# The low part of the token tiles: from a VectorE subtraction to a ScalarE negation and an adding transfer

## The chip, the cores and the metric

One core of one Trainium2 chip runs the kernel. The metric is device time in microseconds (us) of one execution; of the kernel before three runs are given.

## What is computed

The reference takes x of shape 32 x 64 x 1024 (2048 tokens, D = 1024), runs it through a linear map with a gated low-rank addition (8 experts, rank 16, two of them chosen per token), runs the result through a second linear map with another gated low-rank addition (4 experts, rank 8), and adds x. Cut to what matters:

```python
base = einsum('btd,od->bto', x, W)
logits = einsum('btd,ed->bte', x, Wr) + one_hot(language) * 5
topw, topi = top_k(logits, 2); gates = one_hot(topi) . softmax(topw)
h = einsum('btd,erd->bter', x, A)
c = base + 2 * einsum('bter,bte,eor->bto', h, gates, B)
...
gates2 = softmax(einsum('bsi,ei->bse', c, Wr2))
out = x + einsum('bsi,oi->bso', c, W2) + b + 2 * sum_e gates2 * (c A2_e^T Bm_e^T)
```

## The kernel before

The two maps are first multiplied into one (C, with the identity added), which takes about the first 99 us. Then the 2048 tokens go through in 16 tiles of 128, two at a time: eight **pairs**, pair 0 to pair 7. Pairs 0 and 1 have bodies of their own, pairs 2 to 6 are a loop (one body, in which every engine keeps its own order of instructions, written out by hand), pair 7 has the loop's body without what prepares a next pair.

Accuracy comes from splitting. A float32 tile is rounded to the format that TensorE takes (its **high** part), the rest is the **low** part, and a product is three matmuls: high by high, high by low, low by high. So TensorE needs `st_high` and `st_low` of both tiles of a pair (index `odd`, 0 or 1; below "x0" and "x1"), each 128 x 1024, and of four sums and differences of their halves (`s_plain`, hence `s_high` and `s_low`), since a Strassen-like scheme of seven products (P1 to P7) replaces eight.

How a token tile of pair j+1 comes to be, all of it during pair j:

- SP loads it from `tokens` in HBM into `stage[:, odd, :]` (`load_pair`, L461 to L466). It waits until VectorE has made all four sums of the pair that is in `stage` (`s_made`) and until the tile there has been split (`x_split[odd]`). Its transfers x0 and x1 are followed on the same queue by the two stores of the pair (`store`, L468 to L475), which wait for the additions into `rows`.
- ScalarE rounds it, `round_x` (L599 to L601, the copy itself is at L549): x0 once product 2 of pair j is through, x1 once product 4 is.
- VectorE subtracts, `split_x` (L883, the operation itself is at L800), and counts up `x_split[odd]`.
- TensorE uses both parts of pair j+1 from `narrow_products` on (L1494 to L1518), with which a pair of the loop begins: seven products with 244 columns (12 matmuls each), in the order P1n, P6n, P2n, P7n, P5n, P4n, P3n. P1n and P2n read x0; **P4n is the first to read x1**. The wide products with 354 columns follow. In the kernel before, `narrow_products` waits on `x_split[0]` ahead of P1n; ahead of P4n there is only the wait on a sum that VectorE makes later than the split of x1.

```python
pe.wait_ge(x_split[0], j + 1)                                     # ahead of P1n
...
pe.wait_ge(u3n_read, j - 1)                                       # ahead of P4n
narrow_of_x(BANK_NB, 1, 1, tn_high[T4], tn_low[T4], False)
```

POOL (GpSimd) builds a few constants in the first 60 us and then has nothing.

Of the kernel before, what the change touches and what calls it, by code (L numbers as in the profile page):

```python
# [5 lines left out]
def adaln_ffn_kernel(nc, part_2, part_1, part_3, part_4, tokens, gate_proj, mix_rows, language, out):  # L6
# [16 lines left out]
    ALU = mybir.AluOpType  # L23
    ACT = mybir.ActivationFunctionType
# [8 lines left out]
    PAIRS = TILES // 2  # L33
# [56 lines left out]
    with ctx:  # L90
# [3 lines left out]
        def sem(name):  # L94
            return ctx.enter_context(nc.semaphore(name))
# [43 lines left out]
        stage = sb("stage", [P, 2, D])  # L139
# [19 lines left out]
        st_low = sb("st_low", [P, 2, KC, P], F32R)  # L159
# [145 lines left out]
        x_here = [sem("x_here_0"), sem("x_here_1")]  # L305
        x_rounded = [sem("x_rounded_0"), sem("x_rounded_1")]
        x_split = [sem("x_split_0"), sem("x_split_1")]
        s1_made = sem("s1_made")
        s_made = sem("s_made")
        s_rounded = sem("s_rounded")  # L310
# [130 lines left out]
        def sync_program(sp):  # L441


            sp.dma_start(in_2[:, 0, 2 * P:ROWS_A], part_2[0, :, 2 * P:ROWS_A]).then_inc(here_2_first[0], 16)
            sp.dma_start(in_2[:, 0, 0:2 * P], part_2[0, :, 0:2 * P]).then_inc(here_2[0], 16)
            for k in range(1, HALF):
                sp.dma_start(in_2[:, k, :], part_2[k]).then_inc(here_2[k], 16)
            for k in range(HALF):
                sp.dma_start(in_1[:, k, :], part_1[k]).then_inc(here_1[k], 16)
            for k in range(HALF):  # L450
                sp.dma_start(in_3[:, k, :], part_3[k]).then_inc(here_3[k], 16)
            for k in range(HALF):
                sp.dma_start(in_4[:, k, :], part_4[k]).then_inc(here_4[k], 16)
            sp.dma_start(gate_in, gate_proj.rearrange("p k c -> p (k c)")).then_inc(gate_here, 16)
            sp.dma_start(mix_in, mix_rows).then_inc(mix_here, 16)
            sp.dma_start(lang_i[:, :], language).then_inc(lang_here, 16)

            for odd in range(2):
                sp.dma_start(rows[:, odd, :], tokens[odd]).then_inc(x_here[odd], 16)

            def load_pair(j):  # L461

                sp.wait_ge(s_made, 4 * j)
                for odd in range(2):
                    sp.wait_ge(x_split[odd], j)
                    sp.dma_start(stage[:, odd, :], tokens[2 * j + odd]).then_inc(x_here[odd], 16)  # L466

            def store(j):  # L468
                sp.wait_ge(tails_out, j + 1)
                sp.wait_ge(a_out, j + 1)  # L470
                sp.wait_ge(c_out, j + 1)
                sp.dma_start(out[bass.ds(2 * j * P, P), :], rows[:, 0, :]).then_inc(stored[0], 16)
                sp.wait_ge(b_out, j + 1)
                sp.wait_ge(d_out, j + 1)
                sp.dma_start(out[bass.ds((2 * j + 1) * P, P), :], rows[:, 1, :]).then_inc(stored[1], 16)  # L475

            def store_last(j):


                def block_out(t, h):  # L480
                    at = stored_at(h)
                    return sp.dma_start(out[(2 * j + t) * P:(2 * j + t + 1) * P, at], rows[:, t, at])

                def tail_out(t):
                    return sp.dma_start(z_of(out[(2 * j + t) * P:(2 * j + t + 1) * P, :], STORED, HZ),
                                        z_of(rows[:, t, :], STORED, HZ))

                sp.wait_ge(tails_out, j + 1)
                tail_out(0).then_inc(stored[0], 16)
                tail_out(1).then_inc(stored[1], 16)  # L490
                sp.wait_ge(d_out, j + 1)
                block_out(1, 1).then_inc(stored[1], 16)
                sp.wait_ge(b_out, j + 1)
                block_out(1, 0).then_inc(stored[1], 16)
                sp.wait_ge(c_out, j + 1)
                block_out(0, 1).then_inc(stored[0], 16)


            sp.wait_ge(s_split, 4)
            load_pair(1)  # L500


            sp.wait_ge(cw_split, 3)
            sp.wait_ge(t_split, 4)
            for c in (C11, C12, C22, C21):
                k = HALF if c in (C21, C22) else 0
                a = GH if c in (C12, C22) else 0
                sp.dma_start(c_plain[:, c, :, GATE_AT:WIDE], gate_proj[:, k:k + HALF, a:a + GH])\
                    .then_inc(gate_again, 16)
            with sp.Fori(0, PAIRS - 2) as j:  # L510
                load_pair(j + 2)
                store(j)
            store(PAIRS - 2)
            store_last(PAIRS - 1)

        def gpsimd_program(pool):
            nc.gpsimd.memset(ident[:, :], 0.0).then_inc(ident_made, 1)
            pool.wait_ge(ident_made, 1)
            nc.gpsimd.affine_select(out=ident[:, :], in_=ident[:, :], compare_op=ALU.not_equal, fill=1.0,
                                    base=0, pattern=[[-1, P]], channel_multiplier=1).then_inc(ident_made, 1)  # L520
            nc.gpsimd.iota(expert_no[:, :], pattern=[[1, E1]], base=0, channel_multiplier=0,
                           allow_small_or_imprecise_dtypes=True).then_inc(expert_made, 1)

            nc.gpsimd.memset(mix_is_low[:, :], 0.0).then_inc(mask_made, 1)
            pool.wait_ge(mask_made, 1)
            nc.gpsimd.memset(mix_is_low[2 * ER2:3 * ER2, :], 1.0).then_inc(mask_made, 1)
            pool.wait_ge(mask_made, 2)
            nc.gpsimd.affine_select(out=mix_is_low[:, :], in_=mix_is_low[:, :], compare_op=ALU.not_equal, fill=1.0,
                                    base=-(MIX - 1), pattern=[[0, 1]], channel_multiplier=1).then_inc(mask_made, 1)
            pool.wait_ge(mask_made, 3)  # L530
            nc.gpsimd.tensor_scalar(mix_sign[:, :], mix_is_low[:, :], -2.0, 1.0, ALU.mult, ALU.add)\
                .then_inc(mask_made, 1)


            pool.wait_ge(lang_here, 16)
            nc.gpsimd.tensor_copy(lang_f[:, :], lang_i[:, :]).then_inc(lang_made, 1)
            pool.wait_ge(lang_matched, 1)
            nc.gpsimd.tensor_scalar(lang_bias[:, :, :], lang_bias[:, :, :], LANG_BIAS, None, ALU.mult)\
                .then_inc(lang_made, 1)

        def scalar_program(act):

# [5 lines left out]
            def copy(out_, in_):  # L548
                return nc.scalar.activation(out_, in_, ACT.Copy)  # L549
# [49 lines left out]
            def round_x(j, odd, x=stage):  # L599
                act.wait_ge(x_here[odd], 16 * j + 16)  # L600
                copy(st_high[:, odd, :, :].rearrange("p k c -> p (k c)"), x[:, odd, :]).then_inc(x_rounded[odd], 1)  # L601

            def round_s(j, n, plain=s_plain):
                act.wait_ge(s_made, 4 * j + S_MADE[n])
# [16 lines left out]
            for p in range(2):  # L621
                last = copy(c0_sum[:, CUT[p]:CUT[p + 1]], rt_sums(p))
# [74 lines left out]
            def pair(j, first=False, second=False, last=False):  # L697
                steady = not first and not second
# [17 lines left out]
                for t in range(2):  # L716
                    ins = nc.scalar.activation(pair_exp[:, t:t + 1], top[:, t, 0:1], ACT.Exp, bias=top[:, t, 1:2],  # L717
                                               scale=-1.0)
# [13 lines left out]
                if steady and not last:  # L732
                    act.wait_ge(p2_done, j + 1)
                    round_x(j + 1, 0)

                if steady and not last:
                    act.wait_ge(u_half_turned, j - 1)
# [16 lines left out]
                if not steady:  # L754
                    act.wait_ge(p2_done, j + 1)
                    round_x(j + 1, 0)

                act.wait_ge(v_turned, j + 1)
                copy(vt[2 * ER2:3 * ER2, :, :], vt_plain[0:ER2, :, :])
# [9 lines left out]
                if not last:  # L769
                    act.wait_ge(p4_done, j + 1)  # L770
                    round_x(j + 1, 1)

                if not first:
                    act.wait_ge(stored[0], 16 * j)
# [6 lines left out]
                    round_next(j + 1, S1, p5_done)  # L781

            pair(0, first=True)
            pair(1, second=True)
            with act.Fori(2, PAIRS - 1) as j:
                pair(j)
# [6 lines left out]
        def vector_program(dve):  # L793
# [291 lines left out]
            def pair(j, first=False, second=False, last=False):  # L1085
# [181 lines left out]
                    add_r22()  # L1267
                if second:
                    split_tn(T4)
                if not last:  # L1270
                    split_x(j + 1, 0)
                if first:
                    next_s(S1)
# [16 lines left out]
                add_sums(rows[:, 1, wide_at(0)], bank(BANK_B), rows[:, 1, wide_at(0)]).then_inc(b_out, 1)  # L1290
                if turning:
                    split_s(j + 1, S3)
                if not last:
                    split_x(j + 1, 1)
                if first:
                    split_s(j + 1, S2)
# [11 lines left out]
        def tensor_program(pe):  # L1308
# [89 lines left out]
            for n in range(2, STEPS_F):  # L1398
                q, k = of_step(n)
# [58 lines left out]
            def narrow_of_x(n, odd, h, b_high, b_low, fresh):  # L1458
                return narrow_product(n, st_high, st_low, (odd, h * HALF), b_high, b_low, fresh)
# [33 lines left out]

            def narrow_products(j):  # L1494

                pe.wait_ge(x_split[0], j + 1)
                narrow_of_x(BANK_NA, 0, 0, cn_high[B11], cn_low[B11], True).then_inc(p1n_done, 1)

                pe.wait_ge(s_split, 4 * j + S_NO[S2])
# [11 lines left out]
                narrow_of_s(BANK_NC, S1, tn_high[T1], tn_low[T1], True).then_inc(p5n_done, 1)  # L1511

                pe.wait_ge(u3n_read, j - 1)
                narrow_of_x(BANK_NB, 1, 1, tn_high[T4], tn_low[T4], False).then_inc(p4n_done, 1)

                pe.wait_ge(s_split, 4 * j + S_NO[S4])
# [189 lines left out]
```

## Time and profile before

| | |
|---|---|
| median of 3 runs | 323.37 us (322.85, 323.37, 323.40) |
| the profiled execution, span of the core's instructions | 321.9 us |
| difference of the two | 1.5 us |
| TensorE busy | 318.2 us (99%) |
| VectorE busy | 262.5 us (82%) |
| ScalarE busy | 128.2 us (40%) |
| GpSimd busy | 11.3 us (3%) |
| DMA, packets of the transfers queue | 23.5% of 16 engines' span |
| length of one pair of the loop | 27.0 to 27.1 us |

The span is the time from the core's first to its last recorded instruction in one profiled execution; the runs are timed around it, so they are longer by what lies before and after. Busy times of different engines overlap. PE is TensorE's matmul, PEld its weight load, DVE is VectorE, ACT ScalarE, SP and SPq the engine that issues most transfers.

### The profile page before, as it was taken

The numbers are of one execution on the slowest core, as the hardware profiler recorded it, in microseconds if no ns is written. First come the engines' busy times: TensorE is split into PE (matmuls) and PEld (weight loads), VectorE is DVE, ScalarE is ACT, GpSimd is POOL, SyncE is SP. The second block draws the span as 40 slices with busy tenths as digits, with TensorE's granted clock in tenths as the row PEclk, the third lists the DMA queues.
The fourth block names the chain that finished last, engine by engine and source line by source line (L and its number), as shares of the span: only waits on it lengthen the run. The fifth ranks groups of instructions, "written<-read, shape, count | busy, mean of one in ns | idle before, by whom it ended". The sixth has DMA issues, their size and how long they took to land.

```text
span 321.9 us, 5996 instructions
## 1 busy us (share of the span) xinstructions
PE 318.2 (99%) x2246; PEld 311.9 (97%) x2246; DVE 262.5 (82%) x609; ACT 128.2 (40%) x258; POOL 11.3 (3%) x13
## 2 busy tenths in 40 slices
PE   8999999999999999999999999999999999999996
PEld 5999999999999899899999999999999999999996
DVE  3999999798799778988968968878895987888543
ACT  3872836495147236325412503421251350333111
POOL 1001003700000000000000000000000000000000
DMA  7999000000000312700330150051025006002003
GB/s 266 419 404 290 3 2 0 2 0 2 0 2 0 132 24 46 260 3 0 109 154 1 60 201 0 0 191 70 0 74 187 0 21 239 0 0 110 24 0 130
DMA packets 10704, 27.59 MB, mean 86 GB/s; under 512 B 3166, under 2 KB 4702, under 8 KB 10688
## 3 DMA queue, kind: packets, MB, share of 16 engines
q1 hardware_dynamic: 10256, 26.83, 23.5%
q10 hardware_dynamic: 432, 0.53, 0.5%
q8 instruction: 11, 0.18, 0.2%
q14 instruction: 5, 0.04, 0.0%
HBM read 18.97 MB, written 8.39 MB: 85 GB/s over the span
## 4 chain that ended last, share of the span: by engine, by line
PE 98%; DMA 1%; DVE 0%; issue 0%
PE sums L1310 98%; DMA in<-part 1%; PE sums L1571 0%; DVE rows L1069 0%; DVE b_high L806 0%
## 5 line engine op out<-in xcount | busy, mean ns | idle before, releaser
L1310 PE MATMUL sums<-b_high,a_high 128*128 128x256 f32 (+1 forms) x224 | 45.3, 286 | 0.3 <-DVE b_high L806 0.3
L1310 PE MATMUL sums<-b_low,a_high 128*128 128x256 f32 (+1 forms) x224 | 45.2, 286 | 0.0
L1310 PE MATMUL sums<-b_high,a_low 128*128 128x256 f32 (+1 forms) x224 | 45.0, 286 | 0.0
L1310 PEld LDWEIGHTS sums<-b_high,a_high 128*128 128x128 f32 x224 | 34.7, 189 | 1.0 <-ACT a_high L549 0.8
L1310 PEld LDWEIGHTS sums<-b_low,a_high 128*128 128x128 f32 x224 | 34.7, 189 | 0.0
L1310 PEld LDWEIGHTS sums<-b_high,a_low 128*128 128x128 f32 x224 | 34.6, 188 | 0.0
L1310 PE MATMUL sums<-t_high,s_high 128*128 128x354 f32 x96 | 31.3, 326 | 0.0
L1310 PE MATMUL sums<-t_low,s_high 128*128 128x354 f32 x96 | 31.1, 324 | 0.0
L1310 PE MATMUL sums<-t_high,s_low 128*128 128x354 f32 x96 | 31.1, 324 | 0.0
L1069 DVE TENSOR_TENSOR rows<-sums,rows 128x354 f32<-128x354 f32 x48 | 24.4, 522 | 4.1 <-PE sums L1310 3.4
L1310 PE MATMUL sums<-ct_low,st_high 128*128 128x244 f32 (+1 forms) x80 | 25.6, 320 | 0.0
L1310 PE MATMUL sums<-ct_high,st_high 128*128 128x244 f32 (+1 forms) x80 | 25.6, 320 | 0.0
L1310 PE MATMUL sums<-ct_high,st_low 128*128 128x244 f32 (+1 forms) x80 | 25.5, 318 | 0.0
L717 ACT ACTIVATE pair_exp<-top 128x1 f32<-128x1 f32 x16 | 3.8, 287 | 47.9 <-DVE top_at L1157 47.8
L1069 DVE TENSOR_TENSOR narrow<-sums,narrow 128x244 f32<-128x244 f32 x30 | 12.3, 409 | 12.6 <-PE sums L1310 12.6
L1310 PE MATMUL sums<-c_high,st_high 128*128 128x354 f32 x64 | 21.0, 327 | 0.0
L1310 PE MATMUL sums<-c_high,st_low 128*128 128x354 f32 x64 | 20.8, 324 | 0.0
L1310 PE MATMUL sums<-c_low,st_high 128*128 128x354 f32 x64 | 20.7, 324 | 0.0
L800 DVE TENSOR_TENSOR b_low<-in,b_high 128x530 fp32r<-128x530 f32 (+2 forms) x29 | 19.9, 685 | 0.0
L1082 DVE STREAM_TRANSPOSE narrow<-u 32x64 f32<-32x64 f32 x80 | 18.8, 235 | 1.1
L549 ACT ACTIVATE s_high<-s_plain 128x512 fp32r<-128x512 f32 x28 | 16.7, 624 | 7.0 <-PE sums L1310 6.4
L800 DVE TENSOR_TENSOR s_low<-s_plain,s_high 128x512 fp32r<-128x512 f32 x28 | 18.9, 685 | 0.2
(151 smaller groups left out, 845.8 us busy)
## 6 DMA issues: line engine op xcount, KB each, us to landing
stage<-tokens SPq DMA_DIRECT2D x14, 512.0 KB, 4.0
out<-rows SPq DMA_DIRECT2D x14, 512.0 KB, 4.9
in<-part SPq DMA_DIRECT2D x7, 585.0 KB, 8.8
in<-part SPq DMA_DIRECT2D x4, 777.0 KB, 14.0
in<-part SPq DMA_DIRECT2D x4, 265.0 KB, 16.4
rows<-tokens SPq DMA_DIRECT2D x2, 512.0 KB, 13.6
out<-rows SPq DMA_DIRECT2D x3, 192.0 KB, 2.3
c_plain<-gate_proj SPq DMA_DIRECT2D x1, 544.0 KB, 18.0
```

Source lines behind the costliest of these rows:

```text
L549: return nc.scalar.activation(out_, in_, ACT.Copy)
L717: ins = nc.scalar.activation(pair_exp[:, t:t + 1], top[:, t, 0:1], ACT.Exp, bias=top[:, t, 1:2], scale=-1.0)
L800: return nc.vector.tensor_tensor(dst, src, as_f32(high), ALU.subtract)
L1069: return nc.vector.tensor_tensor(dst, n, onto, ALU.add)
L1082: ins = nc.vector.transpose(ut_plain_at(at, q * BLOCK, BLOCK), u[rows_at, :, at])
L1310: return nc.tensor.matmul(out_, lhs, rhs, start=start, stop=stop, skip_group_check=True)
```

## The change

In pairs 1 to 6, which prepare pairs 2 to 7, the low part is no longer made by VectorE. ScalarE, right after it has rounded a token tile, writes minus the tile, rounded as the high part is, into `st_low`: `negate_x` is a Copy with scale -1 from `stage` into the rounded format. Then GpSimd issues a transfer that reads the same tile from `tokens` in HBM once more and adds it onto `st_low` (`accum_op=ADD`), which leaves x minus rounded x. TensorE waits for that transfer (`x_added`). SP's next load waits for the negation in place of the subtraction. Pair 0 is as before, and with it the tiles of pairs 0 and 1. The rest of the difference unrolls one turn of SP's loop.

```diff
-            def load_pair(j):
+            def load_pair(j, steady=False):
                 sp.wait_ge(s_made, 4 * j)
                 for odd in range(2):
-                    sp.wait_ge(x_split[odd], j)
+                    sp.wait_ge(x_negated[odd] if steady else x_split[odd], j)
                     sp.dma_start(stage[:, odd, :], tokens[2 * j + odd]).then_inc(x_here[odd], 16)
...
-            with sp.Fori(0, PAIRS - 2) as j:
-                load_pair(j + 2)
+            load_pair(2)
+            store(0)
+            with sp.Fori(1, PAIRS - 2) as j:
+                load_pair(j + 2, steady=True)
                 store(j)
...
+            for j in range(2, PAIRS):
+                for odd in range(2):
+                    pool.wait_ge(x_negated[odd], j + 1)
+                    pool.dma_start(st_low[:, odd, :, :].rearrange("p k c -> p (k c)"), tokens[2 * j + odd],
+                                   accum_op=ALU.add).then_inc(x_added[odd], 16)
...
+            def negate_x(j, odd):
+                nc.scalar.activation(st_low[:, odd, :, :].rearrange("p k c -> p (k c)"), stage[:, odd, :], ACT.Copy,
+                                     scale=-1.0).then_inc(x_negated[odd], 1)
...
                     act.wait_ge(p2_done, j + 1)
                     round_x(j + 1, 0)
+                    negate_x(j + 1, 0)
...
                     act.wait_ge(p4_done, j + 1)
                     round_x(j + 1, 1)
+                    if not first:
+                        negate_x(j + 1, 1)
...
-                if not last:
+                if first:
                     split_x(j + 1, 0)
...
-                if not last:
+                if first:
                     split_x(j + 1, 1)
...
             def narrow_products(j):
-                pe.wait_ge(x_split[0], j + 1)
+                pe.wait_ge(x_added[0], 16 * (j - 1))
...
                 pe.wait_ge(u3n_read, j - 1)
+                pe.wait_ge(x_added[1], 16 * (j - 1))
                 narrow_of_x(BANK_NB, 1, 1, tn_high[T4], tn_low[T4], False).then_inc(p4n_done, 1)
```

ScalarE's order in the loop's body, from the rounding of x1 to the body's last rounding; before (names are out<-in; the semaphores waited for in brackets):

```order
L549 ACTIVATE vt<-vt_plain 32x256 [waits v_turned]
L549 ACTIVATE vt<-vt_plain 32x256
L604 REGISTER_ALU [waits p7_done]
L549 ACTIVATE s_high<-s_plain 128x512 [waits s_made]
L549 ACTIVATE st_high<-stage 128x1024 [waits x_here_1,p4_done]
L549 ACTIVATE rows<-sums 128x354 [waits a_done,stored_0]
L549 ACTIVATE s_high<-s_plain 128x512 [waits s_made,p5_done]
```

And of the change:

```order
L560 ACTIVATE vt<-vt_plain 32x256 [waits v_turned]
L560 ACTIVATE vt<-vt_plain 32x256
L620 REGISTER_ALU [waits p7_done]
L560 ACTIVATE s_high<-s_plain 128x512 [waits s_made]
L560 ACTIVATE st_high<-stage 128x1024 [waits x_here_1,p4_done]
L616 ACTIVATE st_low<-stage 128x1024
L560 ACTIVATE rows<-sums 128x354 [waits a_done,stored_0]
L560 ACTIVATE s_high<-s_plain 128x512 [waits s_made,p5_done]
```

The negation stands between the rounding of x1 and the copy of product A into `rows`, which everything after it on ScalarE now follows by one instruction more.

TensorE's waits in the narrow products of a loop pair, of the change (the rows between, without waits, are left out by "..."):

```order
L1334 MATMUL sums<-ct_high,st_high 128x244 [waits x_added_0]
...
L1334 MATMUL sums<-ct_high,s_high 128x244 [waits s_split]
...
L1334 MATMUL sums<-ct_high,st_high 128x244 [waits r1n_read]
...
L1334 MATMUL sums<-t_narrow,st_high 128x244 [waits x_added_1,u3n_read]
...
L1334 MATMUL sums<-ct_high,s_high 128x244 [waits r22n_read,s_split]
```

The transfer of x0 is waited for by the first matmul of the pair, that of x1 by the first of P4n, five products later. No matmul moved.

## Rows read from the trace of the kernel before

**Rows 1.** The page's list of engines, and its chain that ended last
```profile
PE 318.2 (99%) x2246; PEld 311.9 (97%) x2246; DVE 262.5 (82%) x609; ACT 128.2 (40%) x258; POOL 11.3 (3%) x13
PE 98%; DMA 1%; DVE 0%; issue 0%
```

**Rows 2.** Busy time by stretch, one pair each: start:end, length, engines, PEclk, DMA share, GB/s
```profile
156.20:183.20 27.00, 27.00 (x193) 27.00 (x192) 21.89 (x68) 7.66 (x20) 0.00 (x0) 1.00 0.22 79
183.20:210.30 27.10, 27.10 (x195) 27.10 (x194) 22.15 (x68) 8.32 (x21) 0.00 (x0) 1.00 0.22 77
```

**Rows 3.** Timeline of PE at the change of pairs: start us, us, what
```profile
210.10 0.33 PE L1310 MATMUL sums<-mix,vt 98*128 98x354 f32 x1
210.27 0.28 PE L1310 MATMUL sums<-ct_high,st_high 128*128 128x244 f32 x1
...
217.10 0.39 PE L1310 MATMUL sums<-t_narrow,st_high 128*128 128x244 f32 x2
```

**Rows 4.** Timeline of ACT in the same pair, in brackets the idle time before
```profile
198.86 1.06 ACT L549 ACTIVATE st_high<-stage 128x1024 fp32r<-128x1024 f32 x1 [1.30 <-PE sums L1310]
199.83 0.29 ACT L549 ACTIVATE ut_high<-narrow 128x128 fp32r<-128x128 f32 x1
201.60 0.31 ACT L549 ACTIVATE ut_high<-narrow 128x128 fp32r<-128x128 f32 x1 [1.49 <-DVE narrow L1082]
...
207.95 1.04 ACT L549 ACTIVATE st_high<-stage 128x1024 fp32r<-128x1024 f32 x1
209.54 0.47 ACT L549 ACTIVATE rows<-sums 128x354 f32<-128x354 f32 x1 [0.55 <-PE sums L1310]
209.91 1.14 ACT L549 ACTIVATE s_high<-s_plain 128x512 fp32r<-128x512 f32 x2
211.83 0.38 ACT L549 ACTIVATE narrow<-sums 128x244 f32<-128x244 f32 x1 [0.78 <-PE sums L1310]
```

**Rows 5.** Timeline of DVE in the same pair
```profile
201.60 0.64 DVE L800 TENSOR_TENSOR ut_low<-narrow,ut_high 128x128 fp32r<-128x128 f32 x2
...
204.01 0.69 DVE L803 TENSOR_TENSOR s_plain<-stage,s_plain 128x512 f32<-128x512 f32 x1
...
211.52 1.22 DVE L800 TENSOR_TENSOR st_low<-stage,st_high 128x1024 fp32r<-128x1024 f32 x1
212.65 0.52 DVE L1069 TENSOR_TENSOR rows<-sums,rows 128x354 f32<-128x354 f32 x1
```

**Rows 6.** The tile st_low: writers by operation, count, ns min/median/max
```profile
L800 DVE TENSOR_TENSOR st_low<-stage,st_high x14: 1214/1219/1227, 124.3 to 293.0; 128x1024 fp32r<-128x1024 f32 x14
```

**Rows 7.** Timeline of SP's queue: the loads of x0 and x1 together, then apart, the stores
```profile
209.45 3.81 SPq L466 DMA_DIRECT2D stage<-tokens  x2
...
212.91 0.35 SPq L466 DMA_DIRECT2D stage<-tokens  x1
213.61 0.35 SPq L472 DMA_DIRECT2D out<-rows  x1
214.22 0.35 SPq L475 DMA_DIRECT2D out<-rows  x1
```

**Rows 8.** DMA issues at 209:212 (x0 alone) and 212.5:213.3 (x1): KB, us to landing
```profile
stage<-tokens SPq DMA_DIRECT2D x1, 512.0 KB, 3.5
...
stage<-tokens SPq DMA_DIRECT2D x1, 512.0 KB, 4.3
```

**Rows 9.** Busy time by stretch of 1 us while x0 is loaded alone (columns as in rows 2)
```profile
210.00:211.00 1.00, 1.00 (x10) 1.00 (x9) 1.00 (x4) 1.00 (x3) 0.00 (x0) 1.00 0.45 106
211.00:212.00 1.00, 1.00 (x12) 1.00 (x11) 1.00 (x3) 0.22 (x2) 0.00 (x0) 1.00 0.88 352
212.00:213.00 1.00, 1.00 (x12) 1.00 (x11) 1.00 (x2) 0.21 (x1) 0.00 (x0) 1.00 0.17 66
```

**Rows 10.** Second store of each pair (L475): DMA to landing
```profile
DMA to landing us min/median/max: 3.5/5.5/6.0
```

More of the change, by code:

```diff
@@ L307, in adaln_ffn_kernel @@
         x_split = [sem("x_split_0"), sem("x_split_1")]
+        x_negated = [sem("x_negated_0"), sem("x_negated_1")]
+        x_added = [sem("x_added_0"), sem("x_added_1")]
         s1_made = sem("s1_made")
@@ L756, in pair @@
                     round_x(j + 1, 0)
+                    if second:
+                        negate_x(j + 1, 0)
                 act.wait_ge(v_turned, j + 1)
@@ L783, in scalar_program @@
             pair(0, first=True)
+            for odd in range(2):
+                act.sem_inc(x_negated[odd], 2)
             pair(1, second=True)
```

## The prediction

> **What bounds the kernel now.** I read the page's list of engines first, then the chain that ended last, then the pairs one by one, then each engine's timeline at the change from one pair to the next. TensorE is busy for 318.2 of 321.9 us and the chain is its own for 98% [rows 1]. A mean over stages could hide a stage that waits for VectorE, so I looked at the pairs alone: in one of 27.0 us matmuls and weight loads both fill all 27.0 us, at a granted clock of 1.00 (the level of 2.4 GHz), while VectorE is busy for 21.9 [rows 2]. The next pair's first matmul, at 210.27, follows the last one's at 210.10 by one matmul's step [rows 3]. So TensorE waits for nobody in the part of the program that the change touches: **no engine can be made fast enough to shorten it**. What can change the time is a new wait of TensorE, and the change makes two, both on transfers. The question is how late each lands against the matmul that needs it.
>
> The chances below speak of 0.2% (0.65 us), about what a measurement of this kernel can tell from no change.
>
> **VectorE loses 12 subtractions**, two in each of pairs 1 to 6, of 1.22 us each [rows 6]: 14.6 us of VectorE. Cost or gain on the path: 0, as TensorE never waits for it [rows 2, 3]. It has one effect aside: the addition of product C, which began at 212.65 right behind the split of x1 [rows 5], begins about 1.1 us earlier, and so does the first store, issued at 213.61 [rows 7]. I return to that.
>
> **ScalarE gains 12 negations.** The nearest row is the rounding of the same tile, 1.04 to 1.06 us, with the next instruction starting 0.97 us after it began [rows 4]; a scale of -1 on the same kind of operation I take at the same price. The first, for x0, runs from 199.83 to 200.88. Behind it waits the first half of `ut_high`, which moves from 199.83 to about 200.8 and ends at 201.1; VectorE wants it at 201.60 [rows 5], and the second half could not begin before 201.60 [rows 4]. Cost 0, with 0.5 us to spare. The second, for x1, runs from 208.92 to 209.97. It moves the copy of product A from 209.54 to about 209.9 and the two roundings behind it by 0.4 us; ScalarE then idles for 0.78 us ahead of 211.83 [rows 4], which takes that up. Cost 0. If that cover were gone, each would cost at most its own 0.97 us per pair.
>
> **SP's loads move forward.** x0 of the next pair but one waited for its tile to be split; now it waits for the last of the four sums, which ends at 204.70 [rows 5], in place of an issue at 209.45 [rows 7]. x1 was issued at 212.91; now it goes at about 210.1, with the negation. That is a gain for nobody, but it moves the traffic: x1's load now sets off at the same moment as the adding transfer of x1, and the stores follow at about 212.5 instead of 213.61.
>
> **The adding transfer of x0** is issued at about 200.9 and is needed at 210.2: 9.3 us. The trace has no adding transfer and none issued by GpSimd. From below I bound it by the load of the same 512 KB alone on the queue, 3.5 us from issue to landing [rows 8]. In it the engines work for 0.45 + 0.88 + 0.17 = 1.50 us [rows 9], so 2.0 us are ahead of the data and behind it. From above I let it fetch two operands (the tokens and `st_low`) one after the other, 1.5 us more, and stand behind x0's load as well, 1.5 us more: 6.5 us. Both fit. Cost 0.
>
> **The adding transfer of x1** decides. Its issue cannot be before 209.97, and P4n's first matmul begins at 217.10 [rows 3], its weight load a little earlier: 7.0 us. The bounds: 3.5 us at the least; at the most 2.0 fixed, 3.0 for two operands, and all of the other traffic of that moment served first, one load and two stores of 1.5 us each: 9.5 us. That traffic costs something shows in x1's load, which took 4.3 us with the stores behind it against 3.5 alone [rows 8], and in the second store, at 5.5 us with the load and the first store about it [rows 10]. Between the bounds I take the two queues to share the engines evenly: 2.0 + 3.0 of its own, and until it is through, the load (1.5) and the first part of the stores, which come to the engines at about 213.5 (1.2). Together **7.7 us, 0.7 us too late**.
>
> On the two operands the Trainium skill ("Collectives: The Full Stack", section on why ReduceScatter is half of AllGather) says that an add in the transfer path is slow not through the arithmetic but because it takes two source reads, on one ring. By that rule the middle value stands; with one read it would be 2.0 + 1.5 + 1.5 = 5.0 us and nothing would be late. No row here shows an adding transfer, so the trace neither agrees nor disagrees.
>
> How often: P4n of pairs 2 to 7 waits, six times. In front of pairs 2 to 6 all this traffic is there; in pair 6 nothing more is loaded, so for pair 7 the transfer has 1.5 us less beside it and fits. A delay of TensorE moves everything that follows with it, so it is neither made up nor does it grow: 5 x 0.7 = 3.5 us. Nothing is due after it: of the tail behind the last matmul nothing changes.
>
> The sum against the profiled execution is 321.9 + 3.5 = 325.4 us; the runs stood 1.5 us above it (323.37), so 326.9 us.
>
> **Rivals.**
>
> *The transfer lands in time* (ends on the other side: no slower). One mechanism, at one place: P4n of each pair, where 7.0 us are to be had. If the adding transfer needs less than 7.0 us, the change costs nothing, and it decides from 0.7 us under my middle value on. For it: one operand read alone gives 5.0 us; even with two, the queues need not share evenly (if the adding one gets two turns for one, the others take 1.5 us from it and it needs 6.5). Against it: 5.5 us for a plain store of the same size with two others about it [rows 10], without a second operand. Time: 323.4, between 322.8 and 324.0. Chance 0.36.
>
> *The adding transfer is slow in itself.* If the engines need 4.5 us or more of work for it (in small pieces, or at the speed of an adder and not of the wire), x1 takes 2.0 + 4.5 + 4.5 = 11.0 us and is 4 us late five times, and in pair 7 about 2.5: 22 us, 346. Down to half of that I count here: 334 to 346. x0 would still fit (2.0 + 4.5 + 1.5 = 8.0 of 9.3). For it: nothing of this kind has a row. Against: nothing either, but plain transfers reach 352 GB/s here [rows 9]. Chance 0.14.
>
> *A gain*. Only a stall that the rows don't show could go. Chance 0.04, 322.0 to 322.7.
>
> *The change does not do what it says*: if VectorE's subtractions stayed or matmuls moved, the order of instructions would show it; it has neither. I give it nothing apart.
>
> **The numbers.** Forecast: slower by a wait ahead of P4n, 0.46, its own range 324.1 to 334. In time 0.36, slow in itself 0.14, gain 0.04. From 322.8 to 335 nearly all of the first two cases lies within, and a little of the third. Faster 0.04, same 0.36, slower 0.60.
>
> **What the profile of the change would show.** If I am right: a new idle time of the weight load or of PE ahead of the first `t_narrow,st_high` matmul of pairs 2 to 6, released by a DMA into `st_low`, of about 0.7 us each; pairs of 27.7 us; and no wait at the first matmul of a pair. DVE busy lower by 14.6, ACT higher by 12.6 us, 6.3 MB more moved from HBM. The landing of the adding transfers is the number to read: 6.5 or less for x0, 7 to 8.5 for x1. Wrong: landings under 7.0 for x1 (then no change), or over 9.5, or a wait at `x_added[0]`, or a wait of SP's stores or of ScalarE that reaches TensorE in the wide products.

## The result and the profile after

| | before | change |
|---|---|---|
| median | 323.38 us (322.85 to 323.49, 4 runs) | 328.43 us (327.89 to 332.45, 4 runs) |
| span of the profiled execution | 321.9 us | 326.9 us |
| its own time | 323.4 us | 328.18 us |

The change is slower: ratio 1.0191, 95% interval 1.0144 to 1.0238. The prediction had 326.9 us with a range of 322.8 to 335.0. The page of the changed kernel, lines for [rows 1] first:

```profile
PE 319.6 (98%) x2246; PEld 312.5 (96%) x2246; DVE 249.3 (76%) x597; ACT 139.0 (43%) x270; POOL 21.6 (7%) x25
...
q1 hardware_dynamic: 10256, 26.83, 23.2%
q0 software_dynamic: 1728, 6.29, 11.4%
...
HBM read 25.26 MB, written 8.39 MB: 103 GB/s over the span
...
PE 82%; DMA 10%; ACT 4%; DVE 2%; issue 2%; ACTq 0%
...
stage<-tokens SPq DMA_DIRECT2D x14, 512.0 KB, 4.0
out<-rows SPq DMA_DIRECT2D x14, 512.0 KB, 6.7
st_low<-tokens POOLq DMA_DIRECT2D x12, 512.0 KB, 6.2
```

VectorE has 13.2 us less to do, ScalarE 10.8 us more, HBM is read for 6.3 MB more (18.97 MB before), and a tenth of the chain that ended last now runs through transfers into `st_low`. TensorE is no longer the chain for 98%.

The 5.0 us by which the span grew are all idle time of TensorE, at two places. The first is the first matmul of pair 2, which reads x0 (timeline of PE and its weight loads, in brackets the idle time before and what ended it):

```profile
157.36 0.19 PEld L1334 LDWEIGHTS sums<-ct_high,st_high 128*128 128x128 f32 x1 [1.58 <-DMA st_low<-tokens]
157.36 0.38 PE L1334 MATMUL sums<-ct_high,st_high 128*128 128x244 f32 x1 [1.28 <-DMA st_low<-tokens]
```

The second is P4n, the first reader of x1, in pairs 2 to 6; pair 7 does not wait:

```profile
165.12 0.30 PEld L1334 LDWEIGHTS sums<-t_narrow,st_high 128*128 128x128 f32 x2 [0.87 <-issue]
165.15 0.46 PE L1334 MATMUL sums<-t_narrow,st_high 128*128 128x244 f32 x2 [0.70 <-DMA st_low<-tokens]
193.32 0.30 PEld L1334 LDWEIGHTS sums<-t_narrow,st_high 128*128 128x128 f32 x2 [1.05 <-issue]
...
221.11 0.30 PEld L1334 LDWEIGHTS sums<-t_narrow,st_high 128*128 128x128 f32 x2 [0.62 <-issue]
...
248.57 0.30 PEld L1334 LDWEIGHTS sums<-t_narrow,st_high 128*128 128x128 f32 x2 [0.29 <-issue]
...
276.36 0.30 PEld L1334 LDWEIGHTS sums<-t_narrow,st_high 128*128 128x128 f32 x2 [0.62 <-issue]
...
303.45 0.31 PEld L1334 LDWEIGHTS sums<-t_narrow,st_high 128*128 128x128 f32 x2
```

The weight load is the record that stops, and shows the whole idle time; the matmul behind it shows 0.17 us less, since the previous matmul is still running. At P4n its idle sums to 0.87 + 1.05 + 0.62 + 0.29 + 0.62 = 3.45 us, and with the 1.58 us at pair 2's start to 5.03 us. Counted from the start of POOL's issue of x1, the transfer had 6.7 to 6.8 us in pairs 3 to 6 and 8.3 us in pair 2, whose products the wait at its start had already pushed back. The name beside the weight load, "issue", says only that no semaphore event stands on that record; the matmul's own record names the DMA.

What is issued in a pair of the loop (POOL's timeline, then SP's, answering to [rows 7]):

```profile
204.59 0.85 POOL L549 DMA_DIRECT2D st_low<-tokens  x1 [18.28 <-ACT st_low L616]
213.65 0.86 POOL L549 DMA_DIRECT2D st_low<-tokens  x1 [8.21 <-ACT st_low L616]
```

```profile
208.30 5.58 SPq L468 DMA_DIRECT2D stage<-tokens  x2
215.72 0.36 SPq L474 DMA_DIRECT2D out<-rows  x1
216.33 0.39 SPq L477 DMA_DIRECT2D out<-rows  x1
```

The two loads are at 208.30 and 213.53. The transfer that adds onto x0 (204.59) has the engines nearly to itself, since SP's load of x0 is issued only 3.7 us behind it, and lands in 5.5 us; that of x1 follows SP's load of x1 by 0.1 us and takes 7.3 us. The stores behind it take 6.6 and 7.2 us here, against 4.9 and 5.5 in the same pair before; TensorE waits for neither. Over the five pairs with a load beside it x1 takes 9.0, 7.8, 7.3, 6.9 and 7.3 us, in pair 6, where nothing more is loaded (for pair 7's tile), 5.6.

### The profile page after: what moved, and what is told of

Same layout as the page of the kernel before. It is cut to its first block, busy times and chain, and to the rows that moved or that the text cites. A ratio compares the mean times of both kernels' runs of the same rounds, so it can differ in the third digit from the quotient of the medians.

```text
span 326.9 us, 6004 instructions
## 1 busy us (share of the span) xinstructions
PE 319.6 (98%) x2246; PEld 312.5 (96%) x2246; DVE 249.3 (76%) x597; ACT 139.0 (43%) x270; POOL 21.6 (7%) x25
## 3 DMA queue, kind: packets, MB, share of 16 engines
q0 software_dynamic: 1728, 6.29, 11.4%
## 4 chain that ended last, share of the span: by engine, by line
PE 82%; DMA 10%; ACT 4%; DVE 2%; issue 2%; ACTq 0%
PE sums L1334 82%; DMA st_low<-tokens 10%; ACT st_low L616 1%; ACT st_high L560 1%; DVE vt_plain L1281 1%; ACT y_exp L767 1%; ACT s_high L560 0%; ACT vt L560 0%; DVE v L1270 0%; DVE sec L1093 0%; PE sums L1596 0%; DVE y_half L1267 0%; DVE rows L1093 0%; DVE y_scale L1268 0%; DVE neg_max L1262 0%
## 5 line engine op out<-in xcount | busy, mean ns | idle before, releaser
L549 POOL DMA_DIRECT2D st_low<-tokens x12 | 10.5, 877 | 224.6 <-ACT st_low L616 224.6
```

Source lines behind the costliest of these rows:

```text
L549: pool.dma_start(st_low[:, odd, :, :].rearrange("p k c -> p (k c)"), tokens[2 * j + odd], accum_op=ALU.add).then_inc(x_added[odd], 16)
```

## The experiments

The theory after the result: the two waits are the whole loss; each adding transfer costs what a second operand costs, and x1's is held up by what else moves at that moment. Against it stood, first, that the price is GpSimd's issue or its queue and not the addition; second, that ScalarE's extra work or the earlier loads cost time by themselves; and of the traffic beside x1, that the stores and not the load hold it up. Each edit below is cut to what matters and shown against the changed kernel, unless it is said otherwise; each ratio is against the kernel before, measured beside it. That kernel stood at 323.37, 323.33 and 323.45 us beside the three sets of four.

### Is it the transfers?

The first kernel leaves the adding transfers out, so that the low part stays minus the rounded tile; TensorE waits for the negation instead.

```diff
-                    pool.wait_ge(x_negated[odd], j + 1)
-                    pool.dma_start(st_low[:, odd, :, :].rearrange("p k c -> p (k c)"), tokens[2 * j + odd],
-                                   accum_op=ALU.add).then_inc(x_added[odd], 16)
...
-                pe.wait_ge(x_added[1], 16 * (j - 1))
+                pe.wait_ge(x_negated[1], j + 1)
```

> Leaves out the adding transfer: the low part stays minus the rounded tile, TensorE waits for the negation. Theory A (the whole 5 us lie in waits for adding transfers; the negations and the missing subtractions are free): 323.4 us, pairs of 27.0 us, no idle time of TensorE ahead of any narrow product. Rival B (ScalarE's 12 negations cost something on the path, 0.97 us each at most): up to 335 us, 325 or more if only some of it shows. Rival C (TensorE did gain from the relief of VectorE, and the transfers hid it): under 322.7.

Measured: 323.06 us, ratio 0.9994 (0.9984 to 1.0003). All of the loss is gone, and nothing is gained beyond. A pair (busy time by stretch, columns as in [rows 2]):

```profile
183.00:210.00 27.00, 27.00 (x193) 27.00 (x192) 19.82 (x66) 9.95 (x23) 0.00 (x0) 1.00 0.23 78
```

Against the second row of [rows 2] VectorE has 2.3 us less to do in the pair and ScalarE 1.6 us more, SP's loads are as early as in the change, and TensorE is as full as before. So the negations and the moved loads cost nothing, and VectorE's relief brings nothing.

The second keeps the transfers and leaves out only the addition (the low part becomes the tile itself).

```diff
-                    pool.dma_start(st_low[:, odd, :, :].rearrange("p k c -> p (k c)"), tokens[2 * j + odd],
-                                   accum_op=ALU.add).then_inc(x_added[odd], 16)
+                    pool.dma_start(st_low[:, odd, :, :].rearrange("p k c -> p (k c)"), tokens[2 * j + odd]).then_inc(x_added[odd], 16)
```

> The same 12 transfers from GpSimd, but as plain copies onto the low part, so that nothing is added (the low part becomes the tile itself). Theory A (the second operand doubles the engines' work): the software queue's share falls from 11.4% to about 5.5% of 16 engines' span, landing of x0 about 4.0 instead of 5.5 us, of x1 about 5.5 instead of 7.3; x1 in time everywhere, x0 of pair 2 needs some 5.1 against 5.3 us to be had: 323.4 to 324. Rival D (issue by GpSimd is what is slow, 0.86 us of it on GpSimd and more behind it): landings within 0.4 us of the adding ones, time 327 to 328.

Measured: 323.39 us, 1.0003 (0.9991 to 1.0015). The tile `st_low`, its issues and landings, then the software queue of the page:

```profile
L549 POOL DMA_DIRECT2D st_low<-tokens x12: 527/528/732, 151.1 to 291.8; - x12
...
DMA to landing us min/median/max: 3.6/4.3/6.4
```

```profile
q0 software_dynamic: 1728, 6.29, 6.3%
```

The same bytes by the same queue at the same moments, without the addition: the engines' share falls from 11.4% to 6.3%, landings of x1 from 6.9 to 9.0 down to 4.9 to 6.4 us, and no matmul waits. GpSimd's issue takes 0.33 us less too (0.53 against 0.86), but x0's landing in the loop got shorter by about 1.8 us, and 1.4 of these are the engines' own work (3.1 us for a transfer, now 1.7). **The addition is the price, not GpSimd's queue.**

### x0 alone, x1 alone

```diff
-                for odd in range(2):
+                for odd in (0,):
...
-                pe.wait_ge(x_added[1], 16 * (j - 1))
+                pe.wait_ge(x_split[1], j + 1)
```

This is the edit for x0 alone; for x1 alone the 0 and the 1 change places. The other tile is split by VectorE as before, and SP's load of it waits for that split.

> Only x0 goes by negation and adding transfer, x1 is split by VectorE as before. Theory A: one wait is left, 1.3 to 1.6 us ahead of the first matmul of pair 2, since in pair 1 the negation of x0 ends only 5.3 us ahead of it, and nothing in the loop: 324.8. If the waits at x1 come from x0's traffic or from the queue as a whole and not from its own transfer: 326 or more.

Measured for x0 alone: 325.4 us, 1.0067 (1.005 to 1.0085). One wait, at the start of pair 2 (timeline):

```profile
157.64 0.19 PEld L1332 LDWEIGHTS sums<-ct_high,st_high 128*128 128x128 f32 x1 [1.82 <-DMA st_low<-tokens]
```

x0 lands in 6.9 us there and in 5.2 to 5.6 elsewhere, where nothing waits. 321.9 + 1.8 + 1.5 is 325.2.

> Only x1 goes by negation and adding transfer, x0 is split by VectorE as before. Theory A: the waits ahead of P4n of pairs 2 to 6 are left, 0.3 to 1.0 us each, that ahead of pair 2 goes: 326.8 (between 326 and 327.3). The costs of the two halves of the change then add up to its 5 us.

Measured for x1 alone: 335.26 us, 1.0356 (1.0336 to 1.0376), over twice the loss of the whole change. A miss, and the most telling one. VectorE still splits x0, late, so SP's loads of x0 and x1 go out together, right ahead of x1's transfer. SP's timeline, POOL's, and the landings of what was issued at 187 to 188:

```profile
186.86 1.01 SPq L468 DMA_DIRECT2D stage<-tokens  x2
```

```profile
187.66 0.87 POOL L549 DMA_DIRECT2D st_low<-tokens  x1 [30.32 <-ACT st_low L616]
```

```profile
stage<-tokens SPq DMA_DIRECT2D x2, 512.0 KB, 4.3
st_low<-tokens POOLq DMA_DIRECT2D x1, 512.0 KB, 9.1
```

With two loads ahead of it the transfer lands in 8.3 to 9.3 us. P4n's first matmuls wait 2.40, 2.19, 1.78, 2.15 and 1.37 us, and its weight loads 10.9 us in all. The profiled execution was longer than the other runs of this kernel (340.57 us against 334.5 to 335.73), with a span of 337.8 us, 15.9 above [rows 1]. The other 5.0 us show in stretches of 1 us, here behind the second wait (columns as in [rows 2]):

```profile
198.00:199.00 1.00, 1.00 (x7) 1.00 (x6) 0.00 (x0) 0.00 (x0) 0.00 (x0) 0.50 0.01 4
...
201.00:202.00 1.00, 1.00 (x9) 1.00 (x8) 0.41 (x1) 0.00 (x0) 0.00 (x0) 1.00 0.00 0
```

After that wait of 2.19 us the granted clock is 0.50 (the level of 1.2 GHz) for 3 to 4 us: fewer matmuls fit into a microsecond. It fell after three of the five waits, not after those of 1.78 and 1.37 us. Three times 3.3 us at half speed, half of it lost, make the 5.0 us. The other four runs had a mean clock of 0.995 against 0.985 in this one; 0.005 of 334 us is 1.7 us, which fits one such stretch in each. They have no profile, so it is argued, not shown, that most of their loss of 11 to 12 us is waits.

### The load or the stores?

Three kernels move traffic away from x1's transfer: SP's load of x1 and the stores behind it wait until it has landed; only the load goes behind the stores; only the stores wait. In all three SP's loop is also written out, turn by turn, which the edits below leave out.

```diff
+                    if steady and odd:
+                        sp.wait_ge(x_added[1], 16 * (j - 2))
```

> SP's load of x1, and with it the two stores behind it on the same queue, wait until the adding transfer of x1 has landed (SP's loop written out, so that the waits are for constants). Theory A (x1 is late through the other traffic): x1 lands after 5.5 to 5.7 us like x0, no wait ahead of P4n in the loop, the wait of pair 2 for x0 stays: 324.9. The stores land about 3 us later, near 222 on the scale of the loop pair read before, where ScalarE wants the rows: if that reaches TensorE, 325.5 to 328. Rival D (the transfer is late by itself): the landing stays at 7 us or more, time 328.

Measured: 343.57 us, 1.0627 (1.0567 to 1.0686). The landing is as expected, 5.2 to 5.4 us for x1 in the loop with nothing beside; the time is not. First the landing of the transfer issued at 219.58, then the waits.

```profile
st_low<-tokens POOLq DMA_DIRECT2D x1, 512.0 KB, 5.2
```

The load that waits is now late for VectorE, and behind VectorE's wait stands an addition that frees a bank for TensorE (waits: in all, times, longest):

```profile
DVE s_plain L935 <- DMA stage<-tokens: 14.8, 4, 3.8
PE sums L1336 <- DVE narrow L1095: 10.3, 4, 2.7
```

The span is 20.4 us above [rows 1]: 10.3 of these waits, 3.1 at the start of pair 2, and a mean granted clock of 0.98, which is 0.02 x 342 = 6.8 us. The kernel repaired one wait and made a worse one.

```diff
-                load_pair(j + 2, steady=True)
+                load_pair(j + 2, steady=True, odds=(0,))
                 store(j)
+                load_pair(j + 2, steady=True, odds=(1,))
```

> SP's load of x1 goes behind the two stores; nothing waits for the adding transfer. The traffic beside x1's adding transfer is still two or three transfers, but begins 2.4 us later (the first store's issue instead of the load's). Theory A with evenly shared engines: own work of 3 us, 2.4 us of it undisturbed, so landing after 6.0 to 6.5 us and no wait in the loop: 324.9. If any traffic at all, or the stores in particular, hold it up: 7 us and more, 326.5 to 328.

Measured: 340.46 us, 1.0529 (1.05 to 1.0558), for the same reason: the load behind the stores lands after 6.4 to 8.6 us. DVE's timeline shows the queue on VectorE, then PE's shows who waited:

```profile
196.35 0.69 DVE L934 TENSOR_TENSOR s_plain<-stage 128x512 f32<-128x512 f32 x1 [3.30 <-DMA stage<-tokens]
196.96 0.40 DVE L1094 TENSOR_TENSOR narrow<-sums,narrow 128x244 f32<-128x244 f32 x1
```

```profile
197.51 0.35 PE L1335 MATMUL sums<-ct_high,s_high 128*128 128x244 f32 x1 [2.17 <-DVE narrow L1094]
```

Still it answers the question: with the two stores issued 1.8 to 2.4 us behind it, and the load only behind them, x1 takes 5.5, 5.3, 5.4, 5.4 and 5.4 us in the loop. The landing of what was issued at 216.40:

```profile
st_low<-tokens POOLq DMA_DIRECT2D x1, 512.0 KB, 5.3
```

**The stores do not hold it up.**

```diff
                 load_pair(j + 2, steady=True)
+                sp.wait_ge(x_added[1], 16 * j)
                 store(j)
```

> Only the two stores of each pair wait until x1's adding transfer has landed; the load of x1 runs beside it. Theory A: load 1.5 us beside own work of 3 us, landing after 6.5 to 7.0 us, which is about what is to be had: 324.9 to 325.8. If the stores do no harm and the load is all: 7.3, 328.

Measured: 329.86 us, 1.0195 (1.0169 to 1.022): no better than the change, a miss. With the load and without the stores x1 takes 7.4, 6.9, 7.9, 7.9 and 8.1 us (5.4 for pair 7, without a load). Issues at 216 to 217 us:

```profile
st_low<-tokens POOLq DMA_DIRECT2D x1, 512.0 KB, 7.9
```

So the load, here issued 0.3 to 0.4 us ahead, is what delays it: 5.4 us without, 6.9 to 8.1 with it. The load pays little in return, 3.9 to 4.2 us against 3.5. What the three kernels do not separate is the kind of the transfer from its moment: the load always went out just ahead, the stores always some 2 us behind, and a load issued 2.7 us or more behind x1's adding transfer did it no harm either (5.3 to 5.5 us).

### Pair 2's first wait

The next kernels leave pair 2's tiles to VectorE, so that the adding transfers begin with pair 3's.

```diff
-            for j in range(2, PAIRS):
+            for j in range(3, PAIRS):
...
+            pair(2, subtracted=True)
+            with pe_loop(3, PAIRS - 1) as j:
```

> Pair 1 prepares pair 2 by VectorE's subtractions as before; negations and adding transfers only in pairs 2 to 6 (pair 2's matmuls written out ahead of the loop). Theory A: both waits of pair 2 go (about 1.3 and 1.0 us), those ahead of P4n of pairs 3 to 6 stay, 0.3 to 1.0 us each: 323.4 + 2.7 = 326.1, between 325.7 and 326.6. If one pair's delay only shifts work to the next: 328.

Measured: 331.39 us, 1.0262 (1.0221 to 1.0303): worse instead of 2.3 better. The edit also took pair 2 out of TensorE's loop, and its waits came out at 1.74, 0.23 and 1.90 us with a further idle time of 1.07 us and a clock of 0.50 at 277 to 280. Two things were changed at once, and the change itself was not measured beside it; nothing follows from it. The pair below was made for that: the change once more, and the edit with TensorE's loop kept, by starting the counters of `x_added` with a tiny transfer.

> The change itself once more, beside the next three on the same chip, since the four kernels before were all slower than expected and had no run of the change beside them. If the chip or the day made no difference: 328.4 us, landings of x1 6.9 to 7.8 in the loop. If that chip served the adding transfers more slowly: 329 or more and landings of 8 us and more.

Measured: 329.38 us, 1.019 (1.0165 to 1.0216), the first result again. In its profile x0 of pair 2 took 7.9 us, not 6.6. The timeline of PE, then the stretches behind it:

```profile
159.46 0.38 PE L1334 MATMUL sums<-ct_high,st_high 128*128 128x244 f32 x1 [2.62 <-DMA st_low<-tokens]
```

```profile
161.00:162.00 1.00, 1.00 (x6) 1.00 (x6) 0.00 (x0) 0.36 (x1) 0.00 (x0) 0.50 1.07 213
162.00:163.00 1.00, 1.00 (x7) 1.00 (x6) 0.00 (x0) 0.01 (x1) 0.00 (x0) 0.50 1.00 250
```

```diff
-                if first:
+                if first or second:
...
+            for odd in range(2):
+                pool.wait_ge(lang_made, 1)
+                pool.dma_start(lang_i[:, :], language).then_inc(x_added[odd], 16)
+                pool.wait_ge(x_added[odd], 16)
+            for j in range(3, PAIRS):
```

> Pair 2's tiles are split by VectorE, adding transfers for pairs 3 to 7 only, with TensorE's loop left as it is (the run before this one that did the same had written out a pair, and showed 1.1 us of idle time of TensorE that the profile puts down to issue). Theory A: both waits of pair 2 go, 2.3 us less than the change run beside it: 326.1. Theory E (a wait of TensorE that is long enough drops its granted clock to the lower level for some us, so that time depends on how long the single waits are, and one landing of 8.5 us costs more than two of 7.3): between 325.5 and 330, with PEclk below 1.00 wherever a wait was over 1.8 us and nowhere else.

Measured: 327.01 us, 1.01 (1.0072 to 1.0128), 2.4 us less than the change beside it. Both waits of pair 2 are gone, that of x0 and that of P4n. What is left is P4n's in pairs 3 to 6 (waits):

```profile
PE sums L1338 <- DMA st_low<-tokens: 2.3, 4, 1.2
```

The longest is 1.4 us on the weight load, and the granted clock is 1.00 behind all four, so this run says nothing on the expectation's second theory, of the clock.

### What of the change is free, and the size of the last wait

The last two edits are shown against the kernel just above.

```diff
-            for odd in range(2):
+            for odd in (0,):
                 pool.wait_ge(lang_made, 1)
```

> Only x0, and only from pair 3 on: half of the change, without the one wait that half had. Theory A: no wait of TensorE at all, 323.4 us, the same as before, with VectorE relieved of 5 subtractions. If anything but the landing of the transfers costs: above 324.

This is the last kernel with x0's transfers alone, x1 being subtracted by VectorE throughout. Measured: 323.66 us, 1.0003 (0.9991 to 1.0015). Tile `st_low`, and a pair of the loop:

```profile
DMA to landing us min/median/max: 5.4/5.4/5.8
```

```profile
187.00:214.00 27.00, 27.00 (x193) 27.00 (x192) 20.78 (x67) 9.22 (x21) 0.86 (x1) 1.00 0.35 97
```

Five adding transfers, none awaited. That part of the change is hidden, and worth nothing: TensorE was full before.

The last kernel gives x1's transfer 0.52 us more by moving one rounding of ScalarE's behind the negation.

```diff
                     negate_x(j + 1, 1)
+                    round_next(j + 1, S3, p7_done)
```

> As e10, and ScalarE's rounding of S3 (0.52 us) goes behind the negation of x1, so that x1's adding transfer is issued 0.52 us earlier. Theory A: each wait ahead of P4n shrinks by 0.5 us or to nothing, 4 x 0.3 to 0.5 us less than e10. Rival F (the load of x1, which moves forward by the same 0.52 us and is served first, is what holds the transfer up): the landing takes as long as in e10 and the gain is the same 0.5 us a wait, since both move together; only if the landing grows by 0.5 us is there no gain.

Measured: 325.71 us, 1.0073 (1.0053 to 1.0092), waits 1.9 us over 3 pairs in place of 2.3 over 4. That is 1.3 us less than the 327.01 us of the kernel it was made from, but the two intervals overlap, and its landings (6.7 to 8.6 us) vary by more than the 0.52 us given. That an earlier issue helps is likely, not settled.

No version here beats the kernel before; the best are equal to it.

## Why the prediction came out right, and where not

**TensorE is the bound, and a new wait is all that can change the time.** Right. Without transfers the same negations, loads and relief gave 323.06 us.

**VectorE less, ScalarE more, both at no cost.** Right on the path. The busy times moved by 13.2 and 10.8 us against 14.6 and 12.6 forecast; consecutive records overlap a little, so a sum of their lengths is too much. By the steps from one record to the next, 1.13 us [rows 5] and 0.97 us [rows 4], it would have been 13.6 and 11.6.

**P4n's wait in pairs 2 to 6, none in pair 7, 3.5 us.** It measured 3.45 us in that profile, on the right records. The middle value of 7.7 us for the landing is within the measured 6.9 to 9.0, but its terms are not all right:

- "2.0 + 3.0 of its own": alone x1 lands in 5.2 to 5.4, so 2.2 to 2.4 us are fixed if the engines' 3.0 hold. They do: 11.4% of 326.9 us over 12 transfers is 3.1 us each, against 1.5 in [rows 9]. The rule of the Trainium skill ("Collectives: The Full Stack", on why ReduceScatter is half of AllGather) is that an add needs two source reads. This trace agrees with it: the transfer without the addition took 6.3% of the engines' span, the one with it 11.4%. No run separates the second read from the rest of what the addition does.
- "the load (1.5)" was the least of what it cost: 1.5 to 2.7 us in the kernel that holds the stores back.
- "the first part of the stores (1.2)" was too much: they cost about nothing.
- "the two queues share the engines evenly" is not what is seen. The load keeps nearly its own time and the adding transfer pays.

The load's price was too low, the stores' too high, and the two errors nearly cancel; that 7.7 us came out near the middle is in part luck. So is the closeness of 3.45 to 3.5 us: 0.87 of it is pair 2, where the transfer took 9.0 us and had 8.3, neither of them the prediction's numbers.

**"The adding transfer of x0 ... Both fit. Cost 0."** This is the step that failed, by 1.6 us of the 5.0. It was worked out from the loop alone, where x0 is negated 9.3 us ahead of its use; there it held in every kernel (5.1 to 5.8 us, no wait). "A wait at `x_added[0]`" was among the prediction's own signs of being wrong. But the tile of pair 2 is made in pair 1, which has a body of its own, and there ScalarE rounds x0 late (its timeline, then POOL's):

```profile
148.41 1.04 ACT L560 ACTIVATE st_high<-stage 128x1024 fp32r<-128x1024 f32 x1
149.36 1.04 ACT L616 ACTIVATE st_low<-stage 128x1024 fp32r<-128x1024 f32 x1
```

```profile
150.71 1.03 POOL L549 DMA_DIRECT2D st_low<-tokens  x1 [88.27 <-ACT st_low L616]
```

The use is due at 155.8 and the negation ends at 150.40, so 5.4 us are to be had, 5.1 of them from POOL's issue on. SP's load goes out at the same moment, and the transfer takes 6.6 us: 1.5 us too long. By the prediction's own prices, 2.0 + 3.0 + 1.5 = 6.5 us, a wait of about 1.1 us would have come out here; the place was not looked at. The price was short as well: in the six profiles with an adding transfer for x0 of pair 2 it landed after 6.6 to 8.1 us, and the wait was up to 3.1. That it is the first transfer of GpSimd's queue is not the reason: in the kernel that starts with pair 3 and has no tiny transfer ahead, the first one has no load beside it until 3.6 us later and lands in 5.3 us. Starting a pair later took 2.4 us off. In the first profile both waits of pair 2 make 1.58 + 0.87 = 2.45 us; in the repetition the first alone was 2.9 us on the weight load, with the slow clock behind it.

**The sum.** 3.45 + 1.58 = 5.03 us for a span that grew by 5.0; forecast 3.5. A third of the loss stood at a place that was priced at nothing. The median lies 1.5 us above the forecast and inside the range and the forecast's own case. The rival that lands in time failed by what the load costs; the one slow in itself did not happen (3.0 us of work, not 4.5).

Left open: why x1 of equal pairs differs, in the loop between 6.7 and 8.7 us over all kernels with one load beside it, and why a load of 1.5 us of work delays it by up to 2.7 with the stores held back (at pair 2 it was 9.0, with x0's own transfer not yet landed); and what makes the run at 332.45 us so long. Its clock was 0.99 over the run, and in the repetition those at 0.995 took 331.2 to 331.5 us against 328.9 to 329.4 at 1.00, which fits a slow stretch behind a long wait. That run has no profile, so this is argued and not shown.

## What to carry to other kernels

A wait that a change adds must be priced in every body of the program in which it occurs, the ones before the loop above all: here the loop's slack of 9.3 us was 5.4 in the body ahead of it. Where one engine fills its time to the last matmul, as TensorE here, work taken off another is worth nothing, and any transfer put in its place can only cost. The adding transfer kept the DMA engines busy for about twice the time of a copy (3.1 us against 1.7), and it was the load issued just ahead of it, not the stores 2 us behind it, that decided when it landed. Holding that load back cost more than it saved, as VectorE and, behind it, TensorE queued for it.

## What the runs showed of the hardware

- 512 KB from HBM added onto a tile: 3.1 us of all 16 engines and 5.1 to 5.8 us to landing with no load ahead of it; copied by the same queue 1.7 us (6.3% over 12) and 3.6 to 3.8 us; loaded by SP's queue 1.5 us and 3.5 us. GpSimd's own record is 0.86 us with the addition, 0.53 without.
- A load issued 0.1 to 0.4 us ahead lengthened the adding transfer in the loop by 1.3 to 3.3 us (from 5.4 to between 6.7 and 8.7) and was itself, without stores, lengthened by 0.4 to 0.7 (from 3.5 to between 3.9 and 4.2); two loads ahead lengthened it by 2.9 to 3.9 us. Two stores 2 us behind it did not (5.3 to 5.5 us).
- After a single wait of TensorE of some 2 us or more the granted clock often fell from 1.00 to 0.50, for 3 to 4 us each time but one (among others after waits of the first matmul of 2.40, 2.19 and 2.15 us with x1 alone, 2.62 in the repetition, 1.90 with pair 2 left out; 6.8 us of slow clock after 2.78 with the stores held). It did not fall after every one: not after 1.78 and 1.74, nor after 2.17 and 2.15 with the load behind the stores, nor after 2.66 with everything held. So the length of the wait alone does not decide it. A stretch of 3.3 us at half the clock costs 1.7 us on top of the wait: in the profiled execution with x1 alone, 10.9 us of waits came with 15.9 us of span.
